# Feed-forward stage of a two-layer graph transformer: three blocks of rows under way instead of two

## Reference, cut to what matters

```python
qkv = layer_norm(x, g1, be1) @ w_qkv
q, k, v = split(qkv)                      # 8 heads of 16
scores = einsum('nhd,mhd->hnm', q, k) * SCALE
attn = softmax(where(adj != 0, scores, -inf), axis=-1)
out = einsum('hnm,mhd->nhd', attn, v).reshape(n, 128)
x = x + out @ w_proj + b_proj
h2 = layer_norm(x, g2, be2)
x = x + gelu(h2 @ w1 + b1) @ w2 + b2      # 128 -> 512 -> 128
```

## Time and profile before

| | |
|---|---|
| median of 3 runs | 3741.22 us (3737.74 to 3742.95) |
| the profiled execution | 3741.04 us |
| its span in the profile | 3739.3 us |
| PE busy over the span | 3467.5 us, 93% |
| DVE, POOL, ACT busy | 2969.6 (79%), 2489.5 (67%), 2334.8 us (62%) |
| feed-forward stage of layer 0 | about 1737 to 1887 us |
| feed-forward stage of layer 1 | about 3586 to 3739 us |

### The profile page before, as it was taken

How to read it: one execution, slowest core, us unless ns; L and a number is a source line. 1 busy time by engine, 2 the same in 40 slices (tenths; PEclk the granted TensorE clock), 3 DMA queues, 4 the chain that set the end, 5 groups by cost and what they waited for, 6 DMA issues and landing times.

```text
span 3739.3 us, 68583 instructions
## 1 busy us (share of the span) xinstructions
PE 3467.5 (93%) x22572; PEld 1404.7 (38%) x22572; DVE 2969.6 (79%) x8997; ACT 2334.8 (62%) x2596; POOL 2489.5 (67%) x1476
## 2 busy tenths in 40 slices
PE   6999999999999999997678999999999999999976
PEld 3443333333333333333434433333333333333234
DVE  6889898888888898841368999999999999999323
ACT  5358686868687777764241466666666666666732
POOL 1067877787878787885010578887878888878930
PEclk9589999999999999998896799999999999999988
DMA  4578787878787878662132546464646565545421
GB/s 137 169 238 259 244 260 236 257 232 263 222 278 221 278 224 281 215 195 76 57 104 87 176 136 190 140 192 139 187 142 183 146 187 147 180 148 175 117 65 51
DMA packets 480351, 676.31 MB, mean 181 GB/s; under 512 B 51552, under 2 KB 272864, under 8 KB 475616
## 3 DMA queue, kind: packets, MB, share of 16 engines
q1 hardware_dynamic: 479568, 671.83, 58.1%
q10 hardware_dynamic: 432, 0.10, 0.0%
HBM read 508.14 MB, written 165.68 MB: 180 GB/s over the span
## 4 chain that ended last, share of the span: by engine, by line
PE 39%; POOL 35%; issue 15%; DVE 7%; DMA 2%; POOLq 1%; ACT 1%; DVEq 0%; SPq 0%; ACTq 0%
POOL arena L921 35%; PE PS L464 12%; PE PS L444 9%; PE PS L477 7%; PE PS L471 6%; DVE spill L798 5%; PE PS L417 3%; POOLq L899 1%; PE PS L450 1%; DVE arena L758 0%; DVE neg_hi L806 0%; DMA arena<-out_dram 0%; PE PS L408 0%; ACT o_sb L673 0%; DMA mask<-in_adj_t 0%
## 5 line engine op out<-in xcount | busy, mean ns | idle before, releaser
L798 DVE CUSTOM_DVE_ANT_0 spill<-PS,mask_n 128x512 bf16<-128x512 f32 x4096 | 2635.8, 688 | 282.2 <-PE PS L444 182.3
L921 POOL TENSOR_TENSOR arena<-arena,mask 128x1024 int32<-128x1024 int32 x896 | 2137.8, 2386 | 646.4 <-ACT arena L665 641.3
L665 ACT ACTIVATE arena<-PS 128x1024 f32<-128x1024 f32 x2048 | 1991.3, 1022 | 919.0 <-PE PS L477 876.4
L444 PE MATMUL PS<-k_t,q_t 48*128 48x512 f32 x4096 | 1287.7, 546 | 61.7 <-DVE pmax L798 41.5
L464 PE MATMUL PS<-arena,v_sb 128*32 128x512 f32 x8192 | 1105.0, 612 | 41.7 <-ACT o_sb L673 37.6
L444 PEld LDWEIGHTS PS<-k_t,q_t 48*128 48x128 f32 x4096 | 546.4, 194 | 1028.8 <-DVE pmax L798 910.9
L471 PE MATMUL PS<-q_t,k_t 50*128 50x512 f32 x4096 | 931.6, 464 | 0.5 <-POOL arena L911 0.4
L477 PE MATMUL PS<-arena,idb 64*128 64x512 bf16 x4312 | 840.9, 390 | 0.0
L471 PEld LDWEIGHTS PS<-q_t,k_t 50*128 50x128 f32 x4096 | 400.2, 188 | 201.9 <-ACT arena L665 123.9
L477 PEld LDWEIGHTS PS<-arena,idb 64*128 64x128 bf16 x4312 | 209.0, 95 | 462.8 <-issue 337.9
L798 DVE DVE_READ_ACCUMULATOR2_ANT pmax<- 128x1 f32 x4096 | 340.1, 83 | 0.0
(11 more groups left out here) (54 smaller groups left out, 970.7 us busy)
## 6 DMA issues: line engine op xcount, KB each, us to landing
mask<-m_dram SPq DMA_DIRECT2D x768, 256.0 KB, 2.7
mask_n<-mn_dram SPq DMA_DIRECT2D x768, 128.0 KB, 2.7
adj_in<-in_adj SPq DMA_DIRECT2D x256, 256.0 KB, 3.8
mask<-in_adj_t SPq DMA_DIRECT2D x256, 256.0 KB, 4.0
m_dram<-mask SPq DMA_DIRECT2D x256, 256.0 KB, 3.7
mn_dram<-mask_n SPq DMA_DIRECT2D x256, 128.0 KB, 3.8
mt_dram<-arena SPq DMA_DIRECT2D x256, 128.0 KB, 3.5
arena<-mt_dram SPq DMA_DIRECT2D x256, 128.0 KB, 2.8
```

The lines of the kernel that those rows point to most:

```text
L444: pe.matmul(bank, q_t[r0:r0 + KROWS, gb % Q_SLOTS, pair, q * P:(q + 1) * P], k_t[r0:r0 + KROWS, pair, mb * TILE:(mb + 1) * TILE], start=Tr ...
L665: nc.scalar.activation(p_buf[:, t % P_SLOTS, 2 * half:2 * half + 2, :], ps_b[:, 2 * half:2 * half + 2, :], ACT.Exp, scale=SCALE).then_inc( ...
L798: dve.tensor_tensor_reduce(spill[:, j % A_BANKS, :], ps_a[:, j % A_BANKS, :], mask_n[:, v % N_SLOTS, :], 1.0, LOWEST, ALU.subtract, ALU.ma ...
L921: pool.tensor_tensor(p, p, m, ALU.mult).then_inc(p_masked, 1)
```

## The change

The feed-forward stage alone is changed, on PE, ACT, DVE and SP; POOL's list is the same. The steps of a block remain the same, instruction for instruction; what moves is which block's steps stand beside each other. While block g goes through both linear layers (steps 6 and 7), block g + 1 is normalised and turned (5), and block g + 2 goes through 1 to 4. Two blocks instead of one run through steps 1 to 3 ahead of the loop. The second layer is split in two halves of 8 matmuls with `turn_attn(g + 2)` between them. `turn_o` waits for the new semaphore `proj_taken` (DVE has read bank 2) where it waited for `x3_ready`. `x2_b` has two buffers. On SP the store of block g - 3 stands behind the loads of block g (it was the store of g - 1), and the loads no longer wait for `x3_ready`.

```diff
--- before.py
+++ after.py
@@ -156,7 +156,7 @@
         attn = carve(NS * P)
         attn_t = carve(TILE)
         x2 = carve(NS * P)
-        x2_b = carve(NS * P)
+        x2_b = carve(2 * NS * P).rearrange("p (s c) -> p s c", s=2)
         x3 = carve(NS * P)
         g_t = carve(4 * TILE).rearrange("p (f c) -> p f c", f=4)
 
@@ -188,7 +188,8 @@
         o_stored = [sem("o_stored_0"), sem("o_stored_1")]
 
         o_loaded, o_turned, attn_ready = sem("o_loaded"), sem("o_turned"), sem("attn_ready")
-        attn_turned, attn_kept, proj_ready = sem("attn_turned"), sem("attn_kept"), sem("proj_ready")
+        attn_turned, attn_kept, proj_ready, proj_taken = (
+            sem("attn_turned"), sem("attn_kept"), sem("proj_ready"), sem("proj_taken"))
         hid_ready, gelu_done, ff_ready, x3_ready, out_stored = (
             sem("hid_ready"), sem("gelu_done"), sem("ff_ready"), sem("x3_ready"), sem("out_stored"))
 
@@ -379,19 +380,17 @@
                         sp.wait_ge(m01_stored[slot], sum(made(0, u) for u in range(slot, STEPS, M_SLOTS)) * 16)
                 phase_barrier(sp, 3 * L + 2)
 
-                for g in range(NB + 1):
+                for g in range(NB + 3):
                     gi, gx = L * NB + g, (2 * L + 1) * NB + g
                     if g < NB:
                         if gi >= 1:
                             sp.wait_ge(o_turned, gi)
                         sp.dma_start(o_in, o_dram[g]).then_inc(o_loaded, 16)
                         sp.wait_ge(xn_ready, gx - 1)
-                        if g >= 1:
-                            sp.wait_ge(x3_ready, gi - 1)
                         sp.dma_start(xt[:, gx % 2], x_rows(g)).then_inc(x_loaded[gx % 2], 16)
-                    if g >= 1:
-                        sp.wait_ge(x3_ready, gi)
-                        sp.dma_start(x_rows(g - 1), x3.rearrange("p (t c) -> p t c", t=NS)).then_inc(out_stored, 16)
+                    if g >= 3:
+                        sp.wait_ge(x3_ready, gi - 2)
+                        sp.dma_start(x_rows(g - 3), x3.rearrange("p (t c) -> p t c", t=NS)).then_inc(out_stored, 16)
                 sp.wait_ge(out_stored, (L + 1) * NB * 16)
                 phase_barrier(sp, 3 * L + 3)
 
@@ -541,7 +540,7 @@
                 pe.wait_ge(o_loaded, (gi + 1) * 16)
                 if gi > 0:
                     pe.wait_ge(attn_kept, gi)
-                    pe.wait_ge(x3_ready, gi - 1 if gi > 1 else 0)
+                    pe.wait_ge(proj_taken, gi)
                 for t in range(NS):
                     for half in range(2):
                         i = 2 * t + half
@@ -577,33 +576,40 @@
                 pe.matmul(PS[:, 4 + f, :], wts[:, C_W1 + f * P:C_W1 + (f + 1) * P], xn_t[:, gx % 2, :],
                           start=True, stop=True).then_inc(hid_ready, 1)
 
-            def second_layer(gi):
-                pe.wait_ge(gelu_done, gi * 4 + 4)
-                if gi > 0:
-                    pe.wait_ge(x3_ready, gi)
-                for t in range(NS):
+            def second_layer(gi, half):
+                if half == 0:
+                    pe.wait_ge(gelu_done, gi * 4 + 4)
+                    if gi > 0:
+                        pe.wait_ge(x3_ready, gi)
+                for t in (2 * half, 2 * half + 1):
                     for f in range(4):
                         mm = pe.matmul(PS[:, 3, t * P:(t + 1) * P], g_t[:, f, t * P:(t + 1) * P],
                                        wts[:, C_W2 + f * P:C_W2 + (f + 1) * P], start=f == 0, stop=f == 3)
-                mm.then_inc(ff_ready, 1)
+                if half == 1:
+                    mm.then_inc(ff_ready, 1)
 
             def feed_forward(L):
-                turn_o(L * NB)
-                turn_attn(L * NB)
-                project_attn(L * NB)
+
+
+                gi0, gx0 = L * NB, (2 * L + 1) * NB
+                for g in range(2):
+                    turn_o(gi0 + g)
+                    turn_attn(gi0 + g)
+                    project_attn(gi0 + g)
+                turn_normed_2(gx0)
                 for g in range(NB):
-                    gi, gx = L * NB + g, (2 * L + 1) * NB + g
-                    turn_normed_2(gx)
+                    for f in range(4):
+                        hidden(gi0 + g, gx0 + g, f)
+                    if g + 2 < NB:
+                        turn_o(gi0 + g + 2)
                     if g + 1 < NB:
-                        turn_o(gi + 1)
-                    for f in range(3):
-                        hidden(gi, gx, f)
-                    if g + 1 < NB:
-                        turn_attn(gi + 1)
-                    hidden(gi, gx, 3)
-                    if g + 1 < NB:
-                        project_attn(gi + 1)
-                    second_layer(gi)
+                        turn_normed_2(gx0 + g + 1)
+                    second_layer(gi0 + g, 0)
+                    if g + 2 < NB:
+                        turn_attn(gi0 + g + 2)
+                    second_layer(gi0 + g, 1)
+                    if g + 2 < NB:
+                        project_attn(gi0 + g + 2)
 
             for L in range(LAYERS):
                 pe.wait_ge(w_here, 16 * (L + 1))
@@ -712,15 +718,17 @@
                                      bias=wts[:, C_B1 + f:C_B1 + f + 1]).then_inc(gelu_done, 1)
 
             def feed_forward(L):
-                keep_attn(L * NB)
+                gi0, gx0 = L * NB, (2 * L + 1) * NB
+                keep_attn(gi0)
+                keep_attn(gi0 + 1)
+                keep_normed(gx0, 0, C_G2, C_BE2)
                 for g in range(NB):
-                    gi, gx = L * NB + g, (2 * L + 1) * NB + g
-                    keep_normed(gx, 0, C_G2, C_BE2)
-                    for f in range(3):
-                        gelu(gi, f)
+                    for f in range(4):
+                        gelu(gi0 + g, f)
                     if g + 1 < NB:
-                        keep_attn(gi + 1)
-                    gelu(gi, 3)
+                        keep_normed(gx0 + g + 1, 0, C_G2, C_BE2)
+                    if g + 2 < NB:
+                        keep_attn(gi0 + g + 2)
 
             for L in range(LAYERS):
                 act.wait_ge(w_here, 16 * (L + 1))
@@ -843,36 +851,36 @@
                 dve.tensor_tensor(attn.rearrange("p (g d) -> p g d", d=HD), rows[:, :, 0:HD],
                                   sums.broadcast_to([P, NS * HEADS, HD]), ALU.mult).then_inc(attn_ready, 1)
 
-            def first_half(gi, gx):
-                normalise(gi)
+            def add_attention(gi, gx):
                 dve.wait_ge(x_loaded[gx % 2], (gx // 2 + 1) * 16)
                 dve.tensor_tensor(x2v, xt[:, gx % 2], row_bias(C_BP), ALU.add)
                 dve.drain()
                 dve.wait_ge(proj_ready, gi + 1)
-                dve.tensor_tensor(x2, PS[:, 2, :], x2, ALU.add)
+                dve.tensor_tensor(x2, PS[:, 2, :], x2, ALU.add).then_inc(proj_taken, 1)
                 dve.drain()
                 norm_stats(x2v, gx)
                 norm_rows(x2v, gx)
-
-            def add_output_bias():
-                dve.tensor_tensor(x2_b.rearrange("p (t c) -> p t c", t=NS), x2v, row_bias(C_B2), ALU.add)
+                dve.tensor_tensor(x2_b[:, gi % 2, :].rearrange("p (t c) -> p t c", t=NS), x2v, row_bias(C_B2), ALU.add)
                 dve.drain()
 
-            def second_half(gi):
+            def add_ff(gi):
                 dve.wait_ge(ff_ready, gi + 1)
                 if gi > 0:
                     dve.wait_ge(out_stored, gi * 16)
-                dve.tensor_tensor(x3, PS[:, 3, :], x2_b, ALU.add).then_inc(x3_ready, 1)
+                dve.tensor_tensor(x3, PS[:, 3, :], x2_b[:, gi % 2, :], ALU.add).then_inc(x3_ready, 1)
                 dve.drain()
 
             def feed_forward(L):
-                first_half(L * NB, (2 * L + 1) * NB)
-                add_output_bias()
-                for g in range(NB - 1):
-                    first_half(L * NB + g + 1, (2 * L + 1) * NB + g + 1)
-                    second_half(L * NB + g)
-                    add_output_bias()
-                second_half(L * NB + NB - 1)
+                gi0, gx0 = L * NB, (2 * L + 1) * NB
+                for g in range(2):
+                    normalise(gi0 + g)
+                    add_attention(gi0 + g, gx0 + g)
+                for g in range(NB):
+                    if g + 2 < NB:
+                        normalise(gi0 + g + 2)
+                    add_ff(gi0 + g)
+                    if g + 2 < NB:
+                        add_attention(gi0 + g + 2, gx0 + g + 2)
 
             for L in range(LAYERS):
                 dve.wait_ge(w_here, 16 * (L + 1))
```

## The result

The changed kernel takes 3658.43 us (median of 4 runs, 3654.05 to 3662.92) against 3739.48 us (3737.36 to 3742.95) before on the same footing: ratio 0.978, 95% interval 0.9765 to 0.9799. It is faster by 81 us. The forecast was 3660 us, 81 us less.

A forecast was written before the change was run, and what follows sets the result against it. The feed-forward stage was taken as a chain of waits: 18.15 us per block, of which 9.75 work. New intervals of 11.1, a longer start and the end gave 39.2 and 41.6 us less by layer: 3660 us, by itself 3644 to 3675.

The forecast's parts named there:

- The interval: Changed feed-forward loop, mid-stage: one block's period, 11.1 us against 18.15 before.
- The reserve ahead of `turn_attn`: Changed loop: DVE's `normalise` ends 0.35 us before PE wants it for `turn_attn`.
- Pause one: Old block: PE's `turn_o` waits 4.7 us for the `o_in` load behind SP's x3 store; forecast to go.
- pause two: Old block: `turn_normed_2` waits 1.26 us for DVE's norm; forecast to stay, at 1.37 us.
- the middle value of 5.1 us: Stage start: block 0's four `hidden`, taken between 3.45 us at high and about 6.9 at low clock.
- the bound of 1.7 us: Stage start: uncertainty from the clock, 1.7 us either way in each layer.
- Block 6: Stage end: no `turn_o` or `turn_attn` beside it; 6.59 + 0.44 + 3.65 = 10.7 us.
- Block 7: Stage end, last block: 4.48 + 3.65 + 0.23 = 8.4 us to the start of x3.
- the low clock's price: Old block: slow stretch at clock 0.50 behind pause one, put at 2.4 us of the 18.15 us interval.
- rival B: Changed stage: clock still falls once a block, between the layers or at pause two; 34 us, 3694 us; chance 0.10.

The follow-up runs named there:

- the kernel with the bias early: The changed kernel with x plus projection bias on DVE moved ahead of the wait for the second layer: 3646.59 us, ratio to before 0.975.
- the repeat: The changed kernel run once more, word for word, on the chip of its variants: 3655.77 us, ratio to before 0.977.
- fill kernel: The kernel before with unread work on PE ahead of `turn_o`: 20 matmuls in one (3715.09 us), 40 transposes in the other (3714.49 us).
- SP's order alone: The kernel before with the x3 store one block later and the x load's wait for x3 removed: 3659.7 us, ratio 0.978.
- the kernel with both edits: The changed kernel with x plus bias early on DVE and `turn_normed_2` behind the first half of `second_layer`: 3644.85 us, ratio 0.974.
- `turn_normed_2` late: The changed kernel with `turn_normed_2` of block g+1 behind the first half of `second_layer(g)`: 3653.1 us (one run).

## Why the prediction was right

- *The interval.* Forecast 11.1, measured 11.07 to 11.09. The loop was the one named: x3, bias, projection's sum, norm, transposes, second layer. In the prediction's terms the sum starts 1.54 us after x3 (I had 0.78 twice, 1.56), and norm to transposes is 4.85 (4.80). The reserve ahead of `turn_attn` was forecast at 0.35 us and is 0.4: `attn` is done at 1782.05, the transposes begin at 1782.48. The kernel with the bias early, whose interval fell by the 0.65 us that the sum came sooner, shows that the loop binds and not merely fits.
- *Pause one goes, pause two stays.* Both seen; pause two is 1.22 us, forecast 1.37.
- *The clock.* It rose near 1755.6 us, 23 us after the stage's first transposes, as forecast (1764 against 1741.6), and stayed. In layer 1 it was 24.6 us, in the repeat 19.1 and 24.5. That the pause and its 12 transposes would not cost the clock is borne out in mid-stage, and the transposes' part by the fill kernel: a pause filled with transposes alone kept 1.00. The Trainium skill (TensorE: Matmul & The Clock Gate, Part 4: PE-mode transpose) says that transposes don't count as busy in the same way and that the full clock doesn't engage for them. By that rule the fill with transposes should have left the clock low; the measurement decides against it here, for float32 transposes among matmuls.
- *Start and end.* First x3 30.2 us after the first transposes by the sum; measured 30.3 in layer 0 and 31.2 in layer 1, where the clock rose later. The chain up to `hidden(0)` was right (it begins 19.5 us after the first transposes, by the sum 19.5), but what the four `hidden` of block 0 take goes by the moment at which the clock rises: 5.45 and 6.06 us in the two layers, and 3.70 in layer 0 of the repeat, whose first x3 came at 28.5. That the middle value of 5.1 us came so near in layer 0 is luck, and the bound of 1.7 us on it was needed. Block 6: 10.7, measured 10.64. Block 7: 8.4 from the end of `second_layer`, which is 8.1 from x3 to x3; measured 8.05.
- *The total.* The stages fell by 39.5 and 40.9 us, sum 80.4, against 39.2 and 41.6, sum 80.8. The profiled execution after is 3654.05 us, 87 less than that before; the 6.6 us beyond the stages lie in stages that the change doesn't touch, and are scatter (below). The medians differ by 81, and that they met the forecast to 2 us is luck in part, since eight runs of the changed kernel spread over 16 us.
- *A part was mis-sized:* the low clock's price was put at 2.4 us per interval as a remainder; the fill kernels give 2.0. The remainder also held small hand-overs between PE's steps: with SP's order alone the clock is 1.00 and no load is late, and the interval of 11.62 is still 0.6 us more than 9.75 of work and 1.27 of pause two. It had no effect on the sum, which was built from the new loop and not by taking away the old parts, but rival B's 3694 would have been 3688.
- *A reading that was wrong:* under rival B stands that a rest of over 4 us comes before each 0.50 in the stage before. One fall of the clock in layer 1 of that same profile comes behind rests of 1.27 and 0.87 us (last section). B was less far off than its argument says.
- *What the prediction had not asked:* it priced three blocks under way against two with the old DMA order, and never the old order of work with the new DMA order. The working already held the terms for it (pause one is a place in SP's queue), and the kernel with SP's order alone shows 96% of the stages' gain.

## What to carry to other kernels

When an engine waits for a load, look first at what stands ahead of that load in the issuing queue: here a store of a late result held up an early load, and one block's shift of that store brought nearly all that a deeper pipeline of all engines did. A pause of TensorE can cost twice, as here, once as a pause and once as low clock behind it (some 4.7 and 2.0 us), and then its removal is worth more than its length; the pause of 1.2 us in mid-stage cost its length alone. After such a change write out the new loop engine by engine: the next late steps were found so, and each was mended by moving one step.

## What was not expected

**The clock can fall in a shorter rest.** In the repeat of the changed kernel the interval of block 6 in layer 0 was 12.27 us instead of 10.64. There is no `turn_o` in that block, and PE rests for 2.08 us ahead of the four transposes:

```profile
1821.80:1828.00 6.20, 4.12 (x14) 1.85 (x14) 4.33 (x16) 2.75 (x4) 1.27 (x2) 1.00 0.14 42
1828.00:1831.50 3.50, 3.50 (x19) 3.50 (x18) 0.07 (x1) 0.78 (x1) 0.00 (x0) 0.52 0.00 0
```

```profile
1821.85 3.60 PE L576 MATMUL PS<-arena,wts 128*128 128x512 f32 x8
1827.53 0.74 PE L568 MATMUL PS<-idf,arena 128*128 128x128 f32 x4 [2.08 <-DVE arena L766]
1828.06 5.33 PE L586 MATMUL PS<-wts,arena 128*128 128x128 f32 x32
```

The clock fell right behind the rest and cost 1.6 us. The same rest left it at 1.00 in the other layer and in both layers of the first profile. So rival B's mechanism is real, once in the four stages profiled of this kernel, and there at a rest of 2.1 us; at the 1.2 us of mid-stage it never appeared.

The kernels in the old order show it at shorter rests still. In their block 7, which has nothing beside it, PE rests for 1.27 us ahead of four transposes and for 0.87 us behind them. In layer 1 of the kernel before:

```profile
3724.14 0.66 PE L569 MATMUL PS<-idf,arena 128*128 128x128 f32 x4 [1.27 <-DVE arena L758]
...
3725.67 5.40 PE L577 MATMUL PS<-arena,wts 128*128 128x512 f32 x8 [0.87 <-ACT arena L627]
```

The same four `hidden` took 3.70 us in layer 0. Of the eight such places (the kernel before, SP's order alone and the two filled ones, two layers each) three lost the clock, with an interval of 11.7 us instead of 10.0: so did layer 1 with SP's order alone and layer 0 with transposes as filling. What decides between the two cases is not shown.

**The totals' scatter comes from attention's clock.** Eight runs of the changed kernel lie between 3648.96 and 3665.09 us, while in its two profiles the feed-forward intervals repeat to 0.03 us and the stages to 0.1. The first `turn_o` of the stage comes at 1741.6 us in the profile before and at 1732.6 after, although nothing ahead of it changed. One stretch of attention, before and after:

```profile
570.00:580.00 10.00, 8.63 (x54) 3.77 (x50) 7.08 (x21) 4.21 (x5) 7.15 (x4) 0.83 0.43 118
```

```profile
570.00:580.00 10.00, 8.65 (x65) 3.61 (x57) 8.54 (x23) 5.52 (x6) 7.16 (x4) 1.00 0.52 153
```

Between 260 and 1720 us the clock falls eight times in the profile before, together 27 us at 0.50, and twice in the profile after, with 7 us. Work of 20 us done at half the speed is 10 us, about the 9 by which the stage begins earlier. The repeat has 17 us at 0.50 and begins at 1737.2, in between. All ten profiles agree: from 3.4 us at 0.50 and a beginning at 1729.4 (the kernel with both edits) to 27.3 us and 1742.1 (`turn_normed_2` late), a straight line through them gives 0.49 us of delay for each us at 0.50. This is read from profiles, not tested by a run that changes attention, and what makes the clock fall there stays open.
